# Residual table-lookup matmuls: an x ring of six fours with a short ring of picks, in place of a ring of four

## The reference

```python
# x: (128, 128, 1024) f32;  itok_B_1_198, itok_B_0_7: one table index per batch
w = L0_cond_weights[itok_B_1_198]          # (B, C, D), table of 200 x 128 x 128
x = x + einsum('bct,bcd->bdt', x, w)
w = L1_cond_weights[itok_B_0_7]            # (B, C, D), table of 8 x 128 x 128
b = fside_8xS_0[itok_B_0_7]                # (B, D)
x = x + einsum('bct,bcd->bdt', x, w) + b[:, :, None]
return x
```

## Time and profile before

| | |
|---|---|
| median of 3 runs | 343.14 us (342.82 to 343.14) |
| the profiled execution | 343.0 us, of which 341.2 us are the span from the first to the last instruction and 1.8 us lie around it |
| granted TensorE clock, mean | 0.952 |
| PE busy | 272.9 us, 80% |
| DVE, ACT, POOL busy | 126.3, 97.0, 65.8 us |
| moved by the core's 16 DMA engines | 140.8 MB |
| the same, mean rate | 413 GB/s |

### The profile page before, as it was taken

How to read it: one execution, slowest core, us unless ns; L and a number is a source line. 1 busy time by engine, 2 the same in 40 slices (tenths; PEclk the granted TensorE clock), 3 DMA queues, 4 the chain that set the end, 5 groups by cost and what they waited for, 6 DMA issues and landing times.

```text
span 341.2 us, 4867 instructions
## 1 busy us (share of the span) xinstructions
PE 272.9 (80%) x774; PEld 131.8 (39%) x774; DVE 126.3 (37%) x202; ACT 97.0 (28%) x135; POOL 65.8 (19%) x249
## 2 busy tenths in 40 slices
PE   1799997678777798786997977889697987978980
PEld 1355443334333354343443433444343443434430
DVE  3145543343333334243442433434243432424440
ACT  1033352232322224132241324313143321323330
POOL 2400311131122211222111222121222111222000
PEclk9999999999999979799897999979799997989996
DMA  7999999999999999999999999999999999999993
GB/s 304 417 409 396 422 430 419 413 423 421 432 434 423 426 422 414 431 424 423 427 427 423 431 430 426 427 421 426 433 426 430 427 429 426 425 426 424 413 387 137
DMA packets 24058, 140.80 MB, mean 413 GB/s; under 512 B 2673, under 2 KB 14322, under 8 KB 15474
## 3 DMA queue, kind: packets, MB, share of 16 engines
q1 hardware_dynamic: 23760, 140.20, 98.7%
q10 hardware_dynamic: 290, 0.53, 0.4%
HBM read 76.03 MB, written 67.11 MB: 419 GB/s over the span
## 4 chain that ended last, share of the span: by engine, by line
DMA 61%; SPq 16%; PE 13%; issue 7%; ACT 0%; DVE 0%; DVEq 0%
DMA out<-xy 54%; PE y_ps L310 11%; SPq L129 9%; SPq L123 5%; DMA xy<-x 4%; DMA w_home<-w_t 2%; PE m_ps L291 2%; SPq L148 2%; ACT xy L406 0%; SPq L162 0%; SPq L151 0%; SPq L203 0%; SPq L156 0%; PE home_ps L324 0%; SPq L176 0%
## 5 line engine op out<-in xcount | busy, mean ns | idle before, releaser
L310 PE MATMUL y_ps<-xy,m_sb 128*128 128x512 f32 x512 | 251.4, 627 | 49.2 <-DMA xy<-x 48.2
L310 PEld LDWEIGHTS y_ps<-xy,m_sb 128*128 128x128 f32 x512 | 94.6, 200 | 155.1 <-issue 155.1
L406 ACT ACTIVATE xy<-y_ps,j_pick 128x512 f32<-128x512 f32 x128 | 88.0, 687 | 227.4 <-PE y_ps L310 227.4
L382 DVE TENSOR_SCALAR xy<-y_ps,j_pick 128x512 f32<-128x512 f32 x128 | 96.1, 751 | 147.9 <-PE y_ps L310 147.9
L242 POOL COPY w_pick<-w_home 128x128 f32 x112 | 33.2, 296 | 238.3 <-issue 238.3
L291 PEld LDWEIGHTS m_ps<-j_pick,w_pick 128*128 128x128 f32 x224 | 35.7, 200 | 30.2 <-issue 29.7
L374 DVE TENSOR_TENSOR m_sb<-m_ps,j_pick 128x256 f32<-128x256 f32 x64 | 27.2, 425 | 47.7 <-PE m_ps L291 46.1
L291 PE MATMUL m_ps<-j_pick,w_pick 128*128 128x128 f32 x224 | 34.9, 279 | 0.0
L244 POOL COPY j_pick<-j_all 128x129 f32 x112 | 33.4, 298 | 0.1
L291 PE MATMUL m_ps<-j_pick,w_home 128*128 128x128 f32 x32 | 5.9, 315 | 6.6 <-DMA w_home<-w_t 6.6
L406 ACT ACT_TABLE_LOAD x7 | 9.0, 1283 | 7.5 <-POOL j_pick L256 7.4
(11 more groups left out here) (16 smaller groups left out, 2.8 us busy)
## 6 DMA issues: line engine op xcount, KB each, us to landing
xy<-x SPq DMA_DIRECT2D x30, 2048.0 KB, 15.1
out<-xy SPq DMA_DIRECT2D x29, 2048.0 KB, 15.0
w_home<-w_t SPq DMA_DIRECT2D x128, 64.0 KB
out<-xy SPq DMA_DIRECT2D x5, 1024.0 KB, 9.7
xy<-x SPq DMA_DIRECT2D x3, 1024.0 KB, 7.7
xy<-x SPq DMA_DIRECT2D x4, 256.0 KB, 13.4
j_all<-w_bias SPq DMA_DIRECT2D x1, 516.0 KB, 3.4
out<-xy SPq DMA_DIRECT2D x2, 256.0 KB, 4.7
```

The source lines that it names most:

```text
L310: nc.tensor.matmul(y_ps[:, b % YB, h, :], m_sb[:, s, k, :], xy[:, s, k, half(h)], start=True, stop=True).then_inc(y_ready, 1)
L382: nc.vector.tensor_scalar(xy[:, s, k, half(0)], y_ps[:, b % YB, 0, :], j_pick[:, s, k, D:D + 1], None, ALU.add).then_inc(left_out[b % YB], 1)
L406: nc.scalar.activation(xy[:, s, k, half(1)], y_ps[:, b % YB, 1, :], ACT.Identity, bias=j_pick[:, s, k, D:D + 1]).then_inc(right_out[b % YB ...
```

## The change

- The ring of x has six fours in place of four (`QUADS = 6`, twelve pairs). 32 fours are five rounds of six and a tail of two fours (`TAIL`, four pairs); before there were eight rounds of four.
- `w0_pick`, `j_pick` and `m_sb` turn in a ring of four pairs (`PB = 4`), apart from that of x. Before picking pair s, POOL waits until both halves of the pair four places before it are brought back from PSUM (`wait_free`), in place of waiting for a store.
- SP's order: the first round loads six fours and 24 W0 blocks in front of everything else (before: four fours and 16 blocks). Only four 0 is stored by pairs. A step now loads the W0 blocks of the four itself and no longer those of the next, issues the store of four n-5, waits for the store of four n-6, and issues the load of four n. After the last load come the stores of fours 27 to 30 and the pieces of 31 (before: 29, 30 and the pieces of 31).
- The loops are written for one and a half times as many pairs; prologues and tails change accordingly.

```diff
-    RING = 8
     QUAD = QB // PAIR
-    QUADS = RING // QUAD
+    QUADS = 6
+    RING = QUADS * QUAD
...
-    AHEAD = QUADS - 1
-    BY_PAIR = 2
+    PB = 4
+    TAIL = PAIRS - ROUNDS * RING
+    END = TAIL - 1
...
-        w0_pick = sb("w0_pick", [C, RING, PAIR, D])
+        w0_pick = sb("w0_pick", [C, PB, PAIR, D])
...
-        j_pick = sb("j_pick", [C, RING, PAIR, D + 1])
-        m_sb = sb("m_sb", [C, RING, PAIR, D])
+        j_pick = sb("j_pick", [C, PB, PAIR, D + 1])
+        m_sb = sb("m_sb", [C, PB, PAIR, D])
...
         def stored_once(r, q):
 
-            return r * 16 + (16 if q < BY_PAIR else 0)
+            return r * 16 + (16 if q == 0 else 0)
...
+            def step(r, q):
+
+                load_w0_of(r, q)
+                store_quad(*((r - 1, q + 1) if q + 1 < QUADS else (r, 0)))
                 sp.wait_ge(stored[q], stored_once(r, q))
                 load_quad(r, q)
...
             sp.wait_ge(home_ready, 4)
-            load_w0(1, 0)
-            store_pair(0, 0)
-            load_w0(1, 1)
-            store_pair(0, 1)
-            load_w0(1, 2)
-            store_pair(0, 2)
-            store_pair(0, 3)
-            load_quad_again(1, 0)
-            load_w0(1, 3)
-            store_quad(0, 2)
-            load_quad_again(1, 1)
-            load_w0_of(1, 2)
-            store_quad(0, 3)
-            load_quad_again(1, 2)
-            load_w0_of(1, 3)
-            with sp.Fori(1, ROUNDS - 1) as r:
-                for q in range(QUADS - 1, 2 * QUADS - 1):
-                    now = (r + q // QUADS, q % QUADS)
-                    after = (r + (q + 1) // QUADS, (q + 1) % QUADS)
-                    load_w0_of(*after)
-                    store_quad(r + (q - AHEAD) // QUADS, (q - AHEAD) % QUADS)
-                    load_quad_again(*now)
-
-            store_quad(ROUNDS - 1, 0)
-            sp.wait_ge(stored[QUADS - 1], stored_once(ROUNDS - 1, QUADS - 1))
-            load_pair(NQ - 1, LAST - 1, x_loaded[QUADS - 1])
+            for s in range(QUAD):
+                store_pair(0, s)
+            with sp.Fori(1, ROUNDS) as r:
+                for q in range(QUADS):
+                    step(r, q)
+
+            step(ROUNDS, 0)
+            load_w0_of(ROUNDS, 1)
+            store_quad(ROUNDS - 1, 2)
+            sp.wait_ge(stored[1], stored_once(ROUNDS, 1))
+            load_pair(NQ - 1, END - 1, last_pair_loaded)
...
-            for q in range(1, QUADS - 1):
+            for q in range(3, QUADS):
                 store_quad(ROUNDS - 1, q)
-            store_pair(ROUNDS - 1, LAST - 1)
+            store_quad(ROUNDS, 0)
+            store_pair(ROUNDS, END - 1)
...
+            def wait_free(r, s):
+
+                n, behind = (r, s - PB) if s >= PB else (r - 1, s - PB + RING)
+                for k in range(PAIR):
+                    b = behind * PAIR + k
+                    pool.wait_ge(left_out[b % YB], n * (ROUND_B // YB) + (b // YB + 1))
+                    pool.wait_ge(right_out[b % YB], n * (ROUND_B // YB) + (b // YB + 1))
+
             def pick(r, s):
 
 
+                wait_free(r, s)
                 pool.wait_ge(w0_loaded[s], r * (PAIR * 16) + PAIR * 16)
...
             with pool.Fori(1, ROUNDS) as r:
                 for s in range(RING):
-
-                    pool.wait_ge(stored[s // QUAD], stored_once(r, s // QUAD))
                     pick(r, s)
+            for s in range(TAIL):
+                pick(ROUNDS, s)
```

More of the change, by code:

```diff
@@ L39, in conditioned_residual_kernel @@
     YB = 2
-    AHEAD = QUADS - 1
-    BY_PAIR = 2
-    assert QUADS == 4 and QUAD == 2 and PAIRS % RING == 0 and HALF <= 512 and RING % MB == 0 and ROUND_B % YB == 0
+    PB = 4
+    TAIL = PAIRS - ROUNDS * RING
+    END = TAIL - 1
+    assert TAIL == 2 * QUAD and HALF <= 512
+    assert RING % MB == 0 and RING % PB == 0 and ROUND_B % YB == 0
     with ExitStack() as ctx:
@@ L102, in half, with slots @@
             return slice(h * HALF, (h + 1) * HALF)
-        def slots(q):
-            return xy[:, q * QUAD:(q + 1) * QUAD, :, :].rearrange("c s k t -> c (s k t)")
+        def slots(s, pairs):
+            return xy[:, s:s + pairs, :, :].rearrange("c s k t -> c (s k t)")
         def quad_of(t, r, q):
@@ L113, in stored_once, with last_out @@
         def stored_once(r, q):
-            return r * 16 + (16 if q < BY_PAIR else 0)
+            return r * 16 + (16 if q == 0 else 0)
+        def last_out(k, h):
+            return out[NQ - 1, :, QB - PAIR + k, half(h)]
         block = ctx.enter_context(nc.Block())
@@ L221, in _ @@
+            store_pair(ROUNDS, END - 1)
             for k in range(PAIR):
-                b = LAST * PAIR + k
-                sp.wait_ge(left_out[b % YB], (ROUNDS - 1) * (ROUND_B // YB) + b // YB + 1)
-                sp.dma_start(out[NQ - 1, :, QB - PAIR + k, half(0)], xy[:, LAST, k, half(0)]).then_inc(last_stored, 16)
+                b = END * PAIR + k
+                sp.wait_ge(left_out[b % YB], ROUNDS * (ROUND_B // YB) + b // YB + 1)
+                sp.dma_start(last_out(k, 0), xy[:, END, k, half(0)]).then_inc(last_stored, 16)
@@ L253, in pick_first @@
                     skip_runtime_bounds_check_because="each word is checked against its own range below")
+                if s >= PB:
+                    wait_free(0, s)
                 for k in range(PAIR):
@@ L289, in product @@
                 for k in range(PAIR):
-                    w0_of_k = w0_home[:, s * PAIR + k, :] if first else w0_pick[:, s, k, :]
+                    w0_of_k = w0_home[:, s * PAIR + k, :] if first else w0_pick[:, s % PB, k, :]
                     last = nc.tensor.matmul(m_ps[:, s % MB, k * D:(k + 1) * D], w0_of_k,
-                                            j_pick[:, s, k, 0:D], start=True, stop=True)
+                                            j_pick[:, s % PB, k, 0:D], start=True, stop=True)
                 last.then_inc(product_ready, 1)
@@ L298, in results @@
                 if k == 0:
-                    if first and s < QUAD:
+                    if last and s >= QUAD:
+                        if s < END:
+                            pe.wait_ge(last_pair_loaded, 16)
+                    elif first and s < QUAD:
                         pe.wait_ge(pair_loaded[s], 16)
-                    elif not last:
+                    else:
                         pe.wait_ge(x_loaded[s // QUAD], r * 16 + (16 if s >= QUAD else 0))
@@ L304, in results @@
                 for h in range(2):
-                    if last:
+                    if last and s == END:
                         pe.wait_ge(last_x_loaded[2 * k + h], 16)
@@ L309, in results @@
                         pe.wait_ge((left_out, right_out)[h][b % YB], r * (ROUND_B // YB) + b // YB)
-                    nc.tensor.matmul(y_ps[:, b % YB, h, :], m_sb[:, s, k, :], xy[:, s, k, half(h)],
+                    nc.tensor.matmul(y_ps[:, b % YB, h, :], m_sb[:, s % PB, k, :], xy[:, s, k, half(h)],
                                      start=True, stop=True).then_inc(y_ready, 1)
@@ L337, in _ @@
                     results(r, s - 1, 1)
+            results(ROUNDS - 1, LAST, 0)
+            product(ROUNDS, 0)
+            results(ROUNDS - 1, LAST, 1)
+            for s in range(1, TAIL):
+                results(ROUNDS, s - 1, 0, last=True)
+                product(ROUNDS, s)
+                results(ROUNDS, s - 1, 1, last=True)
             for k in range(PAIR):
-                results(ROUNDS - 1, LAST, k, last=True)
+                results(ROUNDS, END, k, last=True)
         @block.vector
@@ L373, in sum_m @@
                 dve.wait_ge(product_ready, r * RING + (s + 1))
-                nc.vector.tensor_tensor(m_sb[:, s, :, :],
+                nc.vector.tensor_tensor(m_sb[:, s % PB, :, :],
                                         m_ps[:, s % MB, 0:PAIR * D].rearrange("c (k d) -> c k d", k=PAIR),
-                                        j_pick[:, s, :, 0:D], ALU.add).then_inc(m_ready[s % MB], 1)
+                                        j_pick[:, s % PB, :, 0:D], ALU.add).then_inc(m_ready[s % MB], 1)
             def left(r, s, k):
@@ L381, in left @@
                 dve.wait_ge(y_ready, r * (2 * ROUND_B) + (2 * b + 1))
-                nc.vector.tensor_scalar(xy[:, s, k, half(0)], y_ps[:, b % YB, 0, :], j_pick[:, s, k, D:D + 1], None,
+                nc.vector.tensor_scalar(xy[:, s, k, half(0)], y_ps[:, b % YB, 0, :], j_pick[:, s % PB, k, D:D + 1], None,
                                         ALU.add).then_inc(left_out[b % YB], 1)
             sum_m(0, 0)
-            with dve.Fori(0, ROUNDS - 1) as r:
+            with dve.Fori(0, ROUNDS) as r:
                 for s in range(RING):
@@ L391, in _ @@
                     left(r, s, 1)
[L392 to L396, removed]
+            for s in range(TAIL):
+                left(ROUNDS, s, 0)
+                if s < END:
+                    sum_m(ROUNDS, s + 1)
+                left(ROUNDS, s, 1)
         @block.scalar
@@ L413, in _ @@
                         right(r, s, k)
```

(10 more changed lines are left out.)

27 lines of the change are left out of this document (13 added, 14 removed).

## The result

The changed kernel takes 344.25 us (median of 6 runs, 344.03 to 344.33), the kernel before beside it 342.89 us (6 runs, 342.02 to 343.14). The ratio is 1.0042, interval 1.0029 to 1.0055: 1.4 us slower, small but clear of the 0.2% that can be told. The profiled execution took 344.29 us, 342.5 of them span.

What follows compares the result with a forecast made beforehand. Transfers were taken to bound the kernel, with one lagging DMA engine ending it. The profiled 343.0 us plus 0.20 (W0), 0.35 (reads and writes alone) and 0.3 (code) gave 343.85, forecast as 343.8; range 341.6 to 346.2.

Steps and rivals of the forecast that it cites:

- Parts 1 to 3: SP's load wait keeps its queue depth, late stores don't set the end, PE, DVE, ACT work is covered: 0 us each.
- The hole behind 324: DMA share of 0.68 at 324 to 326, a store waiting for PE: 0.64 us, taken as 0 for the end.
- The rival "faster": The deeper ring frees the transfers; half the last engine's lag and the hole go, 340.6 us; chance 0.14.
- Part 4: POOL's picks wait for the pair four before: nobody waits, 0 us, bound +1 at the start.
- Part 5: SP's W0 loads: 92 blocks move data in place of 91, at 0.20 us a block, +0.20 us.
- Part 6: Longer stretches of only reads at the start and only writes at the end: +0.35 us, bounds 0 and +0.9.
- Part 7: Longer loops and tails: one more code transfer on the last DMA engine, +0.3 us, bounds -0.6 and +1.2.

Runs made afterwards that it cites:

- the second trace of before: The kernel before, unchanged, run and traced again on the same chip: ratio 1.0000, span 341.1 us.
- the second trace at 288.1: The changed kernel, unchanged, run and traced again on the same chip as the kernel before: ratio 1.0045 of before, span 343.5 us.

## Why the prediction came out as it did

The time lies in the range, 0.45 us above the forecast of 343.8. The chances were 0.44 for the same and 0.42 for slower, and it was slower: a sum on the edge, whose last term was too small. The forecast was for 0.7 us more than the 343.14 of before, and 1.4 us more were measured, twice that; that the two times differ by only 0.45 us is in part luck, since the kernel before came out 0.25 us lower beside it.

*Parts 1 to 3, the wait, the late stores, the engines' work, at 0.* Right, and now shown. The load waits as before, landing stays at 15 us (15.2 and 15.5), and the kernel in which the wait is really shortened is slower. The hole behind 324 is gone, and no gain came of it; the second trace of before, with a larger hole and the same end, shows why. PE ends at 322.6, as foreseen (near 323). The rival "faster" is dead: the lag that it hoped to shrink grew.

*Part 4, the picks, at 0 with a bound of +1.* In the changed kernel right (1.0046 with the long ring, 1.0045 with the short one). Alone on the ring of four they cost 0.8 us, within the bound, but not through the waits that I looked for. (From 125.98 to 129.85 two pairs take 1.9 us each, not 2.2; nothing hangs on it.)

*Part 5, W0, +0.20.* 92 blocks as counted, and one more costs about 0.17 us.

*Part 6, reads alone and writes alone, +0.35.* Borne out in the reads, roughly. The packets of the changed kernel over 5 to 38, in which now only reads run, and over 200 to 300:

```profile
DMA packets 4132, 13.41 MB, mean 406 GB/s; under 512 B 460, under 2 KB 3314, under 8 KB 3314
```

```profile
DMA packets 5801, 42.74 MB, mean 427 GB/s; under 512 B 645, under 2 KB 3274, under 8 KB 3274
```

With small packets priced as in part 5 of the prediction, the first is 11.95 MB in 28.5 us, 419 GB/s, the second 41.39 in 95.9, 432: 0.15 us a four, against the 0.12 of the prediction. The figure leans on the price of a small packet: with the 0.17 us a block measured since, the same rows give 409 and 429 GB/s, 0.24 us a four. For the writes alone no kernel isolates the 0.05.

*Part 7, code, "I take one more of them on the last engine, +0.3, bounds -0.6 (two fewer) and +1.2 (four more)".* This is the step that failed in size.
```profile
q1 hardware_dynamic: 15548, 103.60, 101.3%
q8 instruction: 1, 0.02, 0.0%
q14 instruction: 2, 0.02, 0.0%
```

Three code transfers fall into this stretch, at 81.3, 93.4 and 287.5 us, where before had none. They do not come back with each round, so the bodies of six fours are not fetched again. A code transfer can cost the last engine more than the 0.31 us that it takes: at the one of 287.5 the lag goes from 6.19 us to 6.92 between two landings (in the second trace at 288.1 from 6.50 to 7.13), where it otherwise moves by some 0.1. But the kernel before has such a step as well, near 320, and over 120 to 275 no code transfer runs in either kernel: the 1.25 us between the two growths build up there evenly, without any fetching. That was no term of the sum at all. The growth and the terms of parts 5 and 6 together are more than the 1.4 us measured, so they don't simply add, and how the 1.4 us divide is not shown.

That the last engine falls behind faster is shown, in two traces of each kernel. That it does so with the ring of six whichever ring the picks have is shown too. What on the core slows it is not. The number of instructions (growth 1.56 to 1.95), the short ring of picks (2.40) and a deeper queue (3.27 in place of 2.9) go with other growths, longer bodies as such do not, and none of them alone orders the table. The places of the buffers in SBUF changed with every ring and were never varied alone; that rival is untested. This stays open.

## What to carry to other kernels

Before giving a ring more places, ask what lies in the queue while the engine waits for a place. With two transfers still under way, a wait of 100 us in sum is worth nothing, and a shorter one only lets transfers stand longer in line; where the ring is so short that SP waits over an empty queue, it costs 15%. Where transfers fill the whole span, the slowest DMA engine ends the kernel: a longer ring cost 1 to 1.5 us here through that engine, and loop bodies long enough to be fetched again cost 11 us. Waits that only repeat what another engine has waited for already are worth leaving out; here that gave about 0.5 us.

## What was not expected of the hardware

- From 120 us on one of the 16 DMA engines falls behind steadily, by 1.65 us in 155 us in the kernel before and by 2.9 in the changed one, with nearly the same bytes to carry. It is no steady loss from the start: 3.1 and 2.4 us are there already at 66 us in the two traces of before. Three engines in all lag behind the other thirteen (5.3, 2.7 and 2.0 us at 289 us of the first trace).
- A loop body of sixteen pairs makes SP stand for 5.6 us more at each turn than inside the body (7.7 against 2.1), and no wait in the trace names it; only the gap and the two instruction transfers inside it show it.
- Around one instruction transfer of 8 KB the last engine's lag can step up by 0.6 to 0.95 us (before at 319.7 and 317.7 us, changed at 287.5 and 288.1), though the transfer itself takes 0.31 to 0.34 us. Not each one does it: at 93.4 us of the changed kernel the lag moves by 0.1.
- With every W0 block loaded and the conditions gone, the last engine's lag grew by 0.58 us in place of 1.65. Three things changed at once there (37 blocks more, none left out, 320 instructions fewer), so this doesn't say that a load left out costs something.
